# Decoder layer on one core: out-product stages moved later in the query phase, one wait of the state product dropped, value products reordered

## The reference, cut to what matters

```python
qkv = silu(hidden @ qkv_w.T)                     # 32 heads of 128: query, key, value
scores = einsum('bhnd,bhmd->bhnm', cq, ck) * diag_decay
intra  = einsum('bhnm,bhmd->bhnd', scores, cv)
inter  = einsum('bhnd,bhde->bhne', cq * q_decay, kv)
kv_next = kv * block_decay + einsum('bhnd,bhne->bhde', ck * k_decay, cv)
...
normed = norm_w * attn * rsqrt(mean(attn * attn) + EPS)
return sigmoid(hidden @ gate_w.T) * normed @ out_w.T
```

## Time and profile before

| | |
|---|---|
| median of 3 runs | 1916.92 us |
| the profiled execution | 1918.16 us |
| its span, first to last instruction | 1916.3 us |
| granted TensorE clock, mean | 0.989 of full speed |
| busy: PE, DVE, ACT, POOL | 1786.1, 1461.0, 923.4, 641.0 us |

### The profile page before, as it was taken

One profiled execution on the slowest core, in us unless ns is written; L12 is line 12 of the kernel. 1 busy time (PEld: TensorE's weight loads), 2 busy tenths in 40 slices (PEclk: granted clock), 3 DMA queues, 4 the chain that ended last, 5 costly groups with the idle time before them and its releaser, 6 DMA issues.

```text
span 1916.3 us, 27828 instructions
## 1 busy us (share of the span) xinstructions
PE 1786.1 (93%) x9865; PEld 892.0 (47%) x9865; DVE 1461.0 (76%) x2059; ACT 923.4 (48%) x1402; POOL 641.0 (33%) x506
## 2 busy tenths in 40 slices
PE   6999999999999999999999999999999999998887
PEld 4454544445454544445454544445454544574443
DVE  7777777878777777878777777778777777768877
ACT  5554444545454444545453444445453444434664
POOL 2252333324333333334333333424333332302333
PEclk9999999999999999999999999999999999999998
DMA  4212224131423224141422213131322214133332
GB/s 177 73 67 97 75 88 105 63 103 51 127 67 97 75 89 105 49 117 50 125 68 63 76 55 105 50 83 51 94 67 64 75 56 105 56 102 119 110 89 88
DMA packets 158119, 161.54 MB, mean 84 GB/s; under 512 B 99872, under 2 KB 127904, under 8 KB 157600
## 3 DMA queue, kind: packets, MB, share of 16 engines
q1 hardware_dynamic: 146528, 147.09, 25.7%
q0 software_dynamic: 2560, 8.39, 1.4%
q10 hardware_dynamic: 8896, 4.28, 0.8%
HBM read 123.56 MB, written 12.58 MB: 71 GB/s over the span
## 4 chain that ended last, share of the span: by engine, by line
PE 58%; DVE 21%; issue 10%; ACT 8%; DMA 3%; POOL 0%; ACTq 0%; DVEq 0%; POOLq 0%
PE bank L1392 13%; PE bank L1394 13%; PE bank L1393 13%; PE bank L1365 5%; DVE w_pair L1746 4%; DVE acc L1919 3%; PE bank L1479 2%; ACT sig L1643 2%; PE bank L1481 2%; PE bank L1480 2%; DMA v_split<-w_vo 2%; ACT w_pair L1607 2%; DVE gated_split L1746 1%; ACT k_units L1649 1%; DVE bank L1794 1%
## 5 line engine op out<-in xcount | busy, mean ns | idle before, releaser
L1392 PE MATMUL bank<-x_blocks,w_pair 128*128 128x512 f16 (+1 forms) x1820 | 680.4, 374 | 28.6 <-DVE bank L1794 19.9
L1394 PE MATMUL bank<-x_blocks,w_pair 128*128 128x512 f16 (+1 forms) x1820 | 679.8, 374 | 0.0
L1393 PE MATMUL bank<-x_blocks,w_pair 128*128 128x512 f16 (+1 forms) x1820 | 679.8, 374 | 0.0
L2037 POOL TENSOR_TENSOR sums_pair<-raw_pair 128x512 f32<-128x512 f32 x63 | 92.6, 1470 | 632.9 <-DVE w_pair L1746 455.4
L1392 PEld LDWEIGHTS bank<-x_blocks,w_pair 128*128 128x128 f16 x1820 | 178.5, 98 | 235.7 <-DVE bank L1794 34.2
L1394 PEld LDWEIGHTS bank<-x_blocks,w_pair 128*128 128x128 f16 x1820 | 178.7, 98 | 203.8 <-issue 1.4
L1393 PEld LDWEIGHTS bank<-x_blocks,w_pair 128*128 128x128 f16 x1820 | 178.7, 98 | 189.2 <-issue 1.6
L1919 DVE TENSOR_TENSOR acc<-acc,bank 128x512 f32<-128x512 f32 x320 | 209.2, 679 | 18.4 <-PE bank L1481 18.4
L1479 PE MATMUL bank<-w_vo,gated_split 128*128 128x512 f16 x392 | 149.3, 381 | 43.3 <-issue 25.6
L1643 ACT ACTIVATE sig<-bank 128x512 f32<-128x512 f32 x145 | 85.9, 593 | 190.6 <-PE bank L1394 153.3
L2063 POOL TENSOR_TENSOR ssq<-ssq,sig 128x512 f32<-128x512 f32 x64 | 87.3, 1364 | 252.8 <-ACT sig L1665 252.8
(11 more groups left out here) (220 smaller groups left out, 2868.9 us busy)
## 6 DMA issues: line engine op xcount, KB each, us to landing
raw_pair<-w_qk SPq DMA_DIRECT2D x32, 1024.0 KB, 5.6
raw_pair<-w_gate SPq DMA_DIRECT2D x16, 1024.0 KB, 4.9
raw_pair<-w_out SPq DMA_DIRECT2D x16, 1024.0 KB, 4.9
raw_pair<-w_vt SPq DMA_DIRECT2D x15, 1024.0 KB, 4.9
raw_pair<-ctx_in SPq DMA_DIRECT2D x8, 1024.0 KB, 5.0
decay_sb<-rates SPq DMA_DIRECT2D x60, 128.0 KB, 4.6
acc<-x_t SPq DMA_DIRECT2D x4, 1024.0 KB, 11.5
ctx<-raw_pair SPq DMA_DIRECT2D x8, 512.0 KB, 3.6
```

The costliest lines, as they stand in the source:

```text
L1392: pe.matmul(out, w_hi, x_hi, start=unmet and k == 0, stop=False, skip_group_check=halves or not fresh)
L1393: pe.matmul(out, w_hi, x_lo, start=False, stop=False, skip_group_check=halves or not fresh)
L1394: mm = pe.matmul(out, w_lo, x_hi, start=False, stop=k == QT - 1, skip_group_check=halves or not fresh)
L2037: pool.tensor_tensor(s3, a11, a21, ALU.add)
```

## The change

Three edits. In the state product the wait for both turned halves becomes a wait for the half that it reads (`v_first`). In the v phase the order of the products is 1, 7, 6, 2, 4, 5, 3 instead of 1, 7, 6, 4, 2, 5, 3, while the places keep what they hold. In the q phase stages 0, 1 and 2 and the splits of S2, S1 and S4 come one or two products later, and `part(0)` and `part(1)` of the key weights move from behind product 6 to behind products 5 and 4. The diff is whole but for lines that don't change.

```diff
@@ def state(self, g):
-        self.add("state", g=g, bank=bank, free=free, turned=self.k_turned[g], v=[t for b in range(B) for t in self.v_done[b][g]],
+        self.add("state", g=g, bank=bank, free=free, turned=self.k_turned[g], v=self.v_first[g],
                  mm=self.tick("state_mm"), hi=self.tick("st_hi"))
@@ def v_out(self, r):
         if r == 1:
             self.v_done = [[self.v_turned[2:], self.v_turned[:2]] for _ in range(B)]
+            self.v_first = [[self.v_turned[2]], [self.v_turned[0]]]
@@ def end_v(self, v, half):
         self.v_done[v["b"]] = [[done]] * GH
+        self.v_first = [[done]] * GH
@@ def main_part(plan): the q phase where it isn't the last
             "p1": [attend(3), gated(3)] + gate_rest,
-            "p2": sums(S2) + stages(0) + units(3) + split_sum(S2) + sums(S1),
-            "p7": stages(1) + split_sum(S1) + sums(S4) + split_sum(S4),
-            "p6": stages(2) + [part(0), part(1)],
+            "p2": sums(S2) + units(3),
+            "p7": split_sum(S2) + sums(S1) + stages(0) + sums(S4),
+            "p6": split_sum(S1) + stages(1) + split_sum(S4),
+            "p5": stages(2) + [part(0)],
+            "p4": [part(1)],
             "p3": stages(3) + [part(2)],
         }, (1, 2, 6, 7, 5, 4, 3) if last else (1, 2, 7, 6, 5, 4, 3))
@@ the v phase
-        }, (1, 7, 6, 4, 2, 5, 3))
+        }, (1, 7, 6, 2, 4, 5, 3))
```

## The result

| | before | changed |
|---|---|---|
| median (lowest to highest), us | 1916.05 (1914.51 to 1917.29), 4 runs | 1904.23 (1902.17 to 1905.90), 4 runs |
| ratio of the changed kernel, 95% interval | | 0.9938 [0.9921, 0.9955] |
| profiled execution, us | 1918.16 | 1905.90 |
| its span, us | 1916.3 | 1904.0 |
| its mean granted clock | 0.989 | 0.990 |

What follows compares the result with a forecast made beforehand. TensorE, busy 1786 of 1916 us, was taken as the bound, with removed waits often only ends of DVE and ACT chains. 14 x (0.99 + 0.06 + 0) = 14.7 us off 1918.16 gave 1903.5, median 1902.3, range 1887 to 1911.

Steps and rivals of the forecast that it cites:

- edit 1: v phase, new order of the value products: product 4's wait for `u3` goes, c22 follows, -0.99 us in each of 14.
- edit 2: Gate phase, state product waits for one half: 0.97 us go there, only 0.06 us a step is kept.
- `attend(1)` waits instead: Gate phase: TensorE comes 0.97 us earlier and waits 0.91 us for bank 7, released by unit 0's gate multiply.
- edit 3: q phase, stages and splits later: 2.69 us of delays go, 0.81 come, the remaining 1.88 is lost in k; net 0.
- product 7 of q waits: q phase: without stage 0 ahead, product 7 waits 0.81 us for bank 2, released by the second `gate_out`.
- bank copy against the start of q: k phase: stage 4's bank copy ends at 700.6 as before, so TensorE goes on at 700.70, unchanged.
- the 3.7 us: q phase: c22 runs 3.7 us earlier, but two weight halves and two adds in the chain of results eat it.
- rival (d): c22 to bank copy: three splits meet GpSimd's key weight sums, 1.35 us a step net lost, 1936 us; chance 0.05.
- price of 0.8 to 0.9 us for a meeting: DVE: a split of gated values that meets a GpSimd sum takes 0.8 to 0.9 us longer than alone.
- The sum: All steps: 14 x (0.99 + 0.06 + 0) = 14.7 us off the profiled execution's 1918.16, giving 1903.5.
- the four removed waits: TensorE, each step: product 4 of v 0.97, `state(0)` 0.97, stage 1 of q 1.96, product 5 of q 0.73 us.

Runs made afterwards that it cites:

- e1: Kernel before with the new order of the value products alone: 1902.44 us, ratio to before 0.9936.
- e12: The changed kernel run again, unaltered: 1901.03 us, ratio to before 0.9925.
- e5: Changed kernel with part(0) and part(1) of the key weights behind product 6, ahead of c22: 1893.36 us, ratio to before 0.9875.
- e6: Changed kernel with part(0) of the key weights at the start of the q phase, part(1) behind the split of S4: 1889.53 us, ratio to before 0.9863.
- e7: Changed kernel with the two late gates swapped, so that product 7's bank is released first: 1895.71 us, ratio to before 0.9891.
- e10: Changed kernel with the edits of e5 and e7 together: 1892.18 us, ratio to before 0.9880.
- e2: Kernel before with the shorter wait of the state product alone: 1916.52 us, ratio to before 1.0005.
- e11: Changed kernel with the edits of e6 and e7 together: 1889.87 us, ratio to before 0.9863.

## Why the prediction was right

| step of the prediction | forecast | measured |
|---|---|---|
| edit 1, a v phase | -0.99 us | -0.99 (25.52 to 24.53), alone in e1 |
| edit 2, a gate phase | -0.06 us | 0.00 in step 11, -0.05 on average (-0.22 and -0.20 in steps 13 and 14) |
| `attend(1)` waits instead | 0.91 us | 0.83, and 0.06 at `attend(0)` |
| edit 3, q phase, gone | 2.69 us | 1.88 + 0.80 = 2.68 |
| product 7 of q waits | 0.81 us | 0.80 |
| edit 3, k phase, given back | 1.88 us | 1.88 (step 11), 2.08 (step 6) |
| bank copy against the start of q | unchanged | 30.69, before 30.70 us |
| a step | -1.05 us | -0.99 |
| profiled execution | 1903.5 us | 1905.9 |
| median | 1902.3 us | 1904.23; 1901.03 in e12 |

- **Edit 1** was right in place and size, and so was the step on which it hung, that `c22` would follow product 5: 0.99 us from `u3` to `c22` were won. e1 shows that nothing else is needed for the gain.
- **Edit 2** was right that the wait is only the visible end of a chain that ends in unit 0's gate multiply. Of the 0.97 us in the gate phase of step 7, 0.83 came back at `attend(1)` and 0.06 at `attend(0)`; the 0.08 left over is that phase's own gain, 27.36 to 27.29 us. In step 11 the wait was 0.90 us and nothing was left.
- **Edit 3** was right with both terms, the new wait at product 7 and the chain behind `c22`. Adding up DVE's and ACT's queues put the bank copy at 700.6, 30.66 us into the q phase; the run has 30.69, and the links that the prediction names on the way (`c22`, the low halves, the last weight part) are within 0.1 us too. So this was a chain followed, not luck. That the two halves are most of what eats the 3.7 us is shown by e5: with them ahead of `c22` the way from there to the bank copy is 2.63 of those 3.7 us shorter. But the halves are work of the queue wherever they stand, `c22` comes 2.01 us later, and only 0.62 us a step are won; e6, which moves one half out of the queue's busy part, wins 0.80.
- **GpSimd.** In the changed kernel the two halves take 1.22 us each, with no sum beside them, so rival (d) did not come, as forecast. With TensorE half a microsecond earlier alone (e7) it still doesn't; with the halves ahead of `c22` as well (e10) it does. The lock between the two engines that the Trainium skill (SBUF — State Buffer, "Who interferes with whom") describes agrees with e10's rows: the split, which began second, ends 1.08 us behind the end of the sum that it met, so 1.20 of its 2.28 us pass while the sum runs. The forecast's price of 0.8 to 0.9 us for a meeting was too low. It was an average over pairs of splits; the second of the pair at 680.27 by itself takes 1.75 us where one alone takes 0.69:

```profile
681.08 1.75 DVE L1746 SCALAR_TENSOR_TENSOR gated_split<-k_units,gated_split 128x512 f16<-128x512 f32 x1
```

- **The sum** promised 2.4 us too much on the profiled execution. 1.66 us of it is step 15's gate phase at the lower clock, which nothing in the forecast had and which came in some executions only. The other 0.8 us lie in steps 1 to 14, which won 13.9 us instead of 14.7: 13.7 in the v phases (forecast 13.9) and 0.7 in the gate phases (0.8), while q and k together took 0.45 us more (0).
- **A piece of luck** hides in that 0.45. The kernel before's profiled execution lost 0.9 us in the q phase of step 1, which took 28.10 us, in e1 and e2 27.16 and 27.17. Windows of that stretch, columns as above:

```profile
138.00:141.00 3.00, 0.73 (x4) 0.22 (x3) 3.00 (x4) 2.82 (x5) 3.00 (x3) 0.99 0.00 0
141.00:144.50 3.50, 3.50 (x10) 1.21 (x9) 2.76 (x4) 1.06 (x1) 3.34 (x3) 0.52 0.02 5
```

The granted clock was 0.52 behind a pause of 2.27 us. Without that loss q and k would have taken 1.4 us more, nearly all of it in steps 2 to 8, where the forecast, worked out from one step and set at 0, had nothing.
- The median of 1902.3 lies between the two that were measured, 1904.23 and 1901.03. Such closeness says little, since they are 3 us apart themselves; what confirms the mechanism is the phases.

## What to carry to other kernels

A wait that is seen on the busiest engine is worth its length only if the engines behind it follow. Ask of each removed wait which later instruction hangs on the same in-order queue, and follow that queue in the rows to its next meeting with the busy engine; here three of the four removed waits, 3.6 of 4.6 us a step, came back at such a meeting. What paid was other work for TensorE in the place of the wait (e1), work moved on DVE's queue to where DVE stood idle, at least in part (e5, e6), or a better order of releases (e7), and two of these together gave hardly more than the better one (e10, e11). Add up the lengths of all like phases and not of one step alone: small terms of some steps, and of one execution, show only there.

## What the runs showed of the hardware

- A VectorE split of 128 x 1024 took 1.22 us alone and 2.10 (e6) or 2.28 us (e10) where it met a GpSimd sum that had begun before it; both ended 1.08 us behind the end of that sum. In e6 the next GpSimd sum in turn took 2.07 us instead of 1.27. In e5 two splits began 0.58 us behind the end of the last sum and took 2.34 us, no more than alone. An add with one operand in PSUM (the `acc` add at 677.22 of the changed kernel) took 0.67 us beside a sum that ran from 676.71 to 678.42, and 0.67 or 0.68 elsewhere.
- The same delay of 2.19 us at `attend(1)` in eight executions was followed by a lower granted clock in two (0.57 over 4 us in one, 0.70 then 0.87 over 8 us in the other), both times 1.66 us longer, and by full clock in six. Differences of 1 to 3 us between medians here are therefore not read as differences of kernels: the changed kernel gave 1904.23 and, run again, 1901.03.
